# Attention: the high and low parts of the row maxima are made on GpSimd, at the head of its turn, instead of on VectorE

## The reference

```python
scores = jnp.einsum('bqd,bkd->bqk', Q, K) / jnp.sqrt(jnp.float32(D))
attn = jax.nn.softmax(scores, axis=-1)
ctx = jnp.einsum('bqk,bkd->bqd', attn, V)
out = ctx @ wo + bo + x
out = (out - mu) * jax.lax.rsqrt(var + LN_EPS) * gamma + beta
```

## Time and profile before

| | |
|---|---|
| median of 3 runs | 817.22 us (816.66 to 818.12) |
| the profiled execution | 816.08 us, span 813.9 us |
| mean granted TensorE clock | 0.833 |
| TensorE busy | 646.0 us, 79% |
| VectorE busy | 599.6 us, 74% |
| ScalarE busy | 458.5 us, 56% |
| GpSimd busy | 408.8 us, 50% |

### The profile page before, as it was taken

The page is one execution under the profiler, slowest core; times in us unless marked ns, Lnnn a source line. Parts: engine busy times, 40 slices in busy tenths (PEclk is TensorE's granted clock), DMA queues, the critical chain, the costliest instruction groups (busy, mean ns, idle before and its releaser), DMA issues.

```text
span 813.9 us, 16314 instructions
## 1 busy us (share of the span) xinstructions
PE 646.0 (79%) x5121; PEld 283.7 (35%) x5121; DVE 599.6 (74%) x1550; ACT 458.5 (56%) x1057; POOL 408.8 (50%) x559
## 2 busy tenths in 40 slices
PE   4896577632699999999999999999999776667760
PEld 3643455421222222222222232222223533445540
DVE  4788834446878989999899998999983779844430
ACT  5653222210158878888888888888888544222220
POOL 5576778854523234344343443434211448578763
PEclk9997755665579999999999999999999568755665
DMA  7898444325544454454545545455421213443334
GB/s 197 235 252 230 94 75 65 52 24 144 96 87 115 100 116 122 104 128 104 123 113 111 122 102 125 111 112 122 104 58 40 68 29 92 110 88 67 60 42 116
DMA packets 242983, 86.66 MB, mean 106 GB/s; under 512 B 169992, under 2 KB 235688, under 8 KB 242856
## 3 DMA queue, kind: packets, MB, share of 16 engines
q1 hardware_dynamic: 226048, 73.05, 37.8%
q0 software_dynamic: 12288, 10.49, 8.7%
q10 hardware_dynamic: 4584, 2.39, 1.0%
HBM read 56.23 MB, written 31.49 MB: 108 GB/s over the span
## 4 chain that ended last, share of the span: by engine, by line
PE 30%; DVE 26%; POOL 13%; issue 13%; ACT 7%; DMA 7%; SPq 1%; ACTq 0%; POOLq 0%; DVEq 0%
DVE arena L1122 14%; PE psum L1752 8%; PE psum L1743 8%; POOL sums L692 7%; ACT arena L1453 4%; DMA sums<-sums_sb,sidx 4%; POOL arena L667 4%; PE psum L1728 4%; DVE arena L1135 3%; PE psum L1533 2%; DMA arena<-dispatch_rows,arena 1%; DVE arena L1130 1%; PE psum L1692 1%; DVE arena L939 1%; PE psum L1550 1%
## 5 line engine op out<-in xcount | busy, mean ns | idle before, releaser
L1122 DVE TENSOR_REDUCE arena<-psum 128x2 f32<-128x1024 f32 x256 | 306.0, 1212 | 36.3 <-PE psum L1730 36.3
L1453 ACT ACTIVATE arena<-psum 128x512 f32<-128x512 f32 x512 | 278.3, 598 | 72.1 <-PE psum L1743 71.2
L1743 PE MATMUL psum<-arena 122*128 122x512 bf16 x512 | 164.4, 387 | 7.0 <-ACT arena L1453 3.5
L1752 PE MATMUL psum<-arena 128*32 128x512 f32 x1024 | 138.2, 610 | 0.0
L692 POOL DMA_INDIRECT sums<-sums_sb,sidx x64 | 102.0, 1594 | 41.2 <-issue 19.4
L1728 PE MATMUL psum<-arena 48*128 48x512 bf16 x256 | 88.4, 400 | 17.0 <-DMA arena<-qk_parts 7.9
L784 POOL TENSOR_TENSOR arena<-arena 128x128 f32<-128x128 f32 x30 | 14.0, 466 | 149.5 <-DVE arena L1135 149.5
L1730 PE MATMUL psum<-arena 48*128 48x512 bf16 x256 | 88.4, 401 | 0.0
L1743 PEld LDWEIGHTS psum<-arena 122*128 122x128 bf16 x512 | 42.7, 100 | 130.1 <-ACT arena L1453 123.5
L667 POOL DMA_INDIRECT arena<-dispatch_rows,arena x64 | 64.1, 1002 | 27.9 <-issue 17.9
L1610 PE MATMUL psum<-ident,arena 128*128 128x128 f32 x64 | 25.0, 413 | 54.6 <-DMA arena<-dispatch_rows,arena 54.5
(11 more groups left out here) (152 smaller groups left out, 1178.9 us busy)
## 6 DMA issues: line engine op xcount, KB each, us to landing
ctx<-arena SPq DMA_DIRECT2D x32, 256.0 KB, 2.1
arena<-qk_parts SPq DMA_DIRECT2D x127, 64.0 KB
qk_parts<-arena SPq DMA_DIRECT2D x32, 192.0 KB, 3.8
arena<-qk_parts SPq DMA_DIRECT2D x190, 32.0 KB
arena<-qk_parts SPq DMA_DIRECT2D x63, 96.0 KB
arena<-lists SPq DMA_DIRECT2D x16, 256.0 KB, 3.5
sums<-x_sb SPq DMA_DIRECT2D x16, 256.0 KB, 4.6
arena<-ctx SPq DMA_DIRECT2D x64, 64.0 KB, 2.4
```

The source lines that it names most:

```text
L1122: dve.tensor_reduce(mx_r[r % 2][:, p:p + 9:8], src, X, ALU.max).then_inc(a_mx, 1)
L1453: act.activation(p_r[tau % NPB], bank[4 + tau % 2][:, :], ACT.Exp, scale=SCALE).then_inc(a_P, 1)
L1743: pe.matmul(bank[4 + tau % 2][:, :], keys, heads(q_st[r], rows, g), start=True, stop=True)\
L1752: ins = pe.matmul(bank[6][32 * g:32 * g + 32, :], v_r[r][:, g, kt, :], p_r[(4 * kt + g) % NPB], start=(kt == 0), stop=(kt == 3), tile_posi ...
```

## The change

The two functions that make the parts move from VectorE's program into GpSimd's, with the same sizes and operations. GpSimd makes the parts of tile `n + 1` as the first thing of its turn for `n`, ahead of `context(n - 2)`; those of tile 0 ahead of `center(GT, 0)`; those of tiles 29 and 30 ahead of `context(26)` and `context(27)`, and those of tile 31 behind `z_rstd(6)` and ahead of `context(28)`. VectorE no longer makes them at the end of its step; instead its first maximum of tile `t` waits until the low part of tile `t - 2` is made, since the two share a buffer.

```diff
@@ gpsimd, attention()
+                def max_high(t, r):
+                    pool.wait_ge(a_mx, 8 * t + 8)
+                    pool.tensor_copy(mhl_r[r % 2][:, 0:4 * NH], mx_r[r % 2]).then_inc(a_hi, 1)
+
+                def max_low(t, r):
+                    pool.wait_ge(a_hi, t + 1)
+                    pool.tensor_tensor(mhl_r[r % 2][:, 4 * NH:8 * NH], mx_r[r % 2], mhl_r[r % 2][:, 0:4 * NH],
+                                      ALU.subtract).then_inc(a_hl, 1)
+
+                def max_parts(t, r):
+                    max_high(t, r)
+                    max_low(t, r)
                 split(2, 2)
                 split(3, 3)
+                max_parts(0, 0)
                 center(GT, 0)
                 for t in range(GT, NT):
                     n = t - 4
+                    max_parts(n + 1, (n + 1) % NBUF)
                     if n >= 2:
                         context(n - 2, (n - 2) % NBUF)
                     split(t, t % NBUF)
...
                 for t in range(NT - 6, NT - 4):
+                    max_parts(t + 3, (t + 3) % NBUF)
                     context(t, t % NBUF)
                 z_rstd(6)
+                max_parts(NT - 1, (NT - 1) % NBUF)
                 context(NT - 4, (NT - 4) % NBUF)
@@ vector, attention()
                     dve.wait_ge(a_S, 8 * t + (p + 1))
+                    if p == 0:
+                        wait(dve, a_hl, t - 1)
...
-                def max_high(t, r):
-                    dve.wait_ge(a_mx, 8 * t + 8)
-                    dve.tensor_copy(mhl_r[r % 2][:, 0:4 * NH], mx_r[r % 2]).then_inc(a_hi, 1)
-
-                def max_low(t, r):
-                    dve.wait_ge(a_hi, t + 1)
-                    dve.tensor_tensor(mhl_r[r % 2][:, 4 * NH:8 * NH], mx_r[r % 2], mhl_r[r % 2][:, 0:4 * NH],
-                                      ALU.subtract).then_inc(a_hl, 1)
...
-                max_high(0, 0)
-                max_low(0, 0)
                 for p in range(8):
                     row_max(1, 1, p)
-                max_high(1, 1)
-                max_low(1, 1)
...
-                    if n + 2 < NT:
-                        max_high(n + 2, at(2))
-                        max_low(n + 2, at(2))
                     if n >= 2:
                         z_stats(n - 2)
```

## The result

The changed kernel takes 850.6 us in the median of four runs (848.1 to 851.6), the one before 817.7 (816.7 to 819.4, four runs on the same chip): a ratio of 1.040, 95% interval 1.037 to 1.043. Predicted were 853 and a range of 838 to 868. The profiled execution after took 851.3 us with a span of 849.6.

What follows compares the result with a forecast made beforehand. The bound was taken to be the chain of hand-overs between TensorE and VectorE in the attention. 816.1 us plus 29.6 of waits and 6.6 of clock falls gave 852.3, with the median 1.1 higher: 853, range 838 to 868.

Steps and rivals of the forecast that it cites:

- The first root's wait: TensorE's transpose of the maxima at 304.74, behind GpSimd's root (L772, L774): 2.88 us lost, once in four steps.
- the pair: The two moved instructions (L1126, L1130) on GpSimd: 0.38 us each, 0.84 us together with 0.08 to start.
- Gamma: Transpose at 317.35, behind GpSimd's product with gamma (L780): 0.68 us late, making VectorE's third maximum 0.41 us late.
- The second root: Transpose at 330.09, behind GpSimd's root (L620, L622): 1.97 us late, 0.24 got back, 1.73 left.
- The laps: Four attention steps running, 50.75 us before: each lap loses 4.61 us to waits, 27.7 us in six.
- the last root: GpSimd's L774 at 608.15 to 609.19, ahead of the last moved instructions: the transpose loses 1.90 us.
- The clock: TensorE's clock falls to half in the attention in four of six laps, 1.65 us each, 6.6 us.
- the clock holds: Rival: same waits in the attention, but TensorE's clock does not fall, 847 us; chance 0.27.
- 13 falls: Rival: TensorE's clock falls to half after each of the 13 long stalls, 868 us; chance 0.12.
- Plain steps stay: Steps where GpSimd is idle: moved instructions end at 342.5, before TensorE's 343.07; nothing lost, steps stay at 12.4 us.
- the stall beside gamma: VectorE's L1130 takes 1.26 us, not 0.17, beside GpSimd's L780; ending it gains at most 1.1 us a lap.
- The rival of a faster kernel: Freed VectorE decides: L1130's stall beside L780 goes, 1.1 us in each of six laps, 811 us; chance 0.04.

Runs made afterwards that it cites:

- two kernels of the experiments: Changed kernel, its two instructions made ahead of GpSimd's roots and product with gamma, 813.5 us; kernel before, that product waiting for VectorE's low part, 813.9 us.

## Why the prediction was right, point by point

- *The place in GpSimd's order costs, not GpSimd.* Right, and shown: the same pair one place earlier gives 813.5 us.
- *The first root's wait.* Forecast 2.88 us, measured 2.56 as TensorE's idle time and 2.62 in the distance (15.04 - 12.42). The mis-sized term is the pair: from the root's end (308.71) to the transpose (309.29) it took 0.58 us, where the sum had 0.84. The 128x16 instructions of 0.20 and 0.22 us cost no more than the 128x4 one of 0.23; the value taken between that and the 128x128 one was too high.
- *Gamma.* Forecast 0.68 us late; TensorE's wait is 0.38, less mainly by the 0.26 of the pair, and the distance grew by 0.50 (13.12 against 12.62).
- *The second root.* Forecast 1.97 us late against the rhythm of the kernel before, of which 1.73 left. By the distances the transpose is 0.50 + 1.15 = 1.65 late, of which TensorE, late itself by then, sees 1.22 as a wait; 0.13 is got back (12.84 against 12.97), where 0.24 was forecast, and 1.52 is left. The transpose is thus 0.32 us less late than forecast, 0.26 of it the pair.
- *The laps.* Forecast 4.61 us each without the clock, measured 2.62 + 1.52 = 4.14 (54.89 - 50.75). Forecast for the last root 1.90, measured 1.1 (the last distance, 13.02 against 11.88).
- *The clock.* Forecast a fall in four of six laps at 1.65 us, 6.6 in all; measured five, of 1.26 to 1.50, together 6.8. That the two sums agree is luck: there was one fall more, and each was cheaper. In the lap without a fall the same 2.56 us wait stands, so how many falls come was a guess and stays one. The likelier rival (the clock holds) fell, and so did the other (13 falls): after waits of 1.22 us it never fell.
- *The sum.* By the medians the change costs 33.0 us; the forecast had 36. The parts found in the trace are 24.8 for the waits in six laps, 6.8 for the falls and 1.1 for the last root, 32.7. The forecast's waits, 29.6, were 3.7 too dear, by the pair above all. That the profiled execution came within 1 us of its forecast (851.3, 852.3) is luck too: its span is 35.7 us longer, and 2.9 of that are 0.5 between the first transpose and the laps, 1.4 ahead of the first transpose and 1.0 behind the last. These need not be the change's. The kernel with gamma behind the pair does there just what the kernel before does (first transpose at 217.7), and has its first transpose at 217.9 in one profile and 215.8 in the other.
- *Plain steps stay.* Right: 12.42 us before and after in the steps ahead of the first lap, and 0.7 us of room measured. The reading had 342.5 against 343.07, 0.6.
- *The gain on VectorE.* The prediction gave the stall beside gamma "1.1 us at most, once a lap", taking the lap's whole surplus over four plain steps, 1.07, for it. The bound held but the sizing was poor: it is 0.29. Another 0.25 of the surplus goes with the pair in the distance of the plain step, and what makes up the remaining half was not tested; the small work of VectorE's two full steps is the likely owner. The rival of a faster kernel was thus over-priced at 811; two kernels of the experiments came to 814.
- *The signs.* The laps (54.9 to 56.4 us), the pair right behind the roots and the product with gamma, the stall gone and VectorE idle ahead of its third maximum (1.09 us in gamma's step) came as said. One missed: the wait two steps after the long one was to be 1.5 to 2 us and is 1.22.

Still open: why one lap in six has no fall after the same wait, what the gamma wait is worth in the whole time, and what the last half microsecond of the lap's surplus is.

## What to carry to other kernels

Work that moves to an in-order engine inherits every wait ahead of it in that engine's program, so read the end of the turn before the place, not only the load of the engine: GpSimd was idle half the time, and the pair of 0.5 us cost 33 us behind waits that were harmless until then. When something on the chain is given to an engine with slack, put it ahead of what waits for things made later; here that turned 1.040 into 0.997. And a stall of an engine is worth only what the next wait behind it leaves over: 0.29 of 1.09 us here.

## What the runs showed of the hardware that was not expected

- TensorE's clock fell from its full level to 1.2 GHz at a wait of 2.56 us between dense matmuls in five of six laps (and in one of six it did not), in each of two kernels, and it never fell at waits of 1.22 us, in four kernels. In the first lap the dense stretch from 309.1 to 312.3 ran at half clock, the one from 312.5 at full. One fall of ten lasted twice as long as the others and cost 2.26 us instead of 1.2 to 1.5. Matmuls without use in the wait prevented the falls and made the kernel faster by about 1% (ratios 1.029 and 1.040).
- A small GpSimd instruction is hardly slower than VectorE's when it stands alone: 0.20 and 0.22 us for 128x16 against 0.17. In a row the gap is wider: eight independent copies took 0.14 us each from start to start on GpSimd (1.10 us), four on VectorE 0.08 (0.32 us).
- VectorE's instruction with two inputs in SBUF was held for the whole of GpSimd's product, 1.26 us instead of 0.17, and took 0.17 to 0.21 in all places once the two no longer met. The prediction had this much; what it had not is that the stall's 1.09 us were worth 0.29 us a lap. By the Trainium skill, "SBUF — State Buffer", section "Who interferes with whom", two SBUF inputs on VectorE contend with a GpSimd instruction that reads SBUF; the trace agrees.
